# The embedding's bias by a spreading transfer instead of a one-row matmul

## The reference

```python
patches = x[:, idx, :].reshape(B, starts.shape[0], P * F)
return jnp.einsum('bnp,dp->bnd', patches, W) + b          # b has 512 values
h = h + _L0_attn_ref(_layernorm(h, axis=-1), ...)         # ternary weights, quantised activations
h = h + _L0_ffn_ref(_layernorm(h, axis=-1), ...)          # 16 experts
h = h + _L1_attn_ref(_layernorm(h, axis=-1), ...)         # causal attention
h = h + _L1_ffn_ref(_layernorm(h, axis=-1), ...)          # gated, with Hadamard rotations
```

## Time and profile before

| | |
|---|---|
| median of 3 runs | 303.21 us (302.82, 303.21, 305.16) |
| the profiled execution | 305.13 us, span of its instructions 303.3 us |
| PE, DVE, ACT, POOL busy | 277.0, 237.1, 145.0, 14.4 us |
| mean granted clock of PE over the span | 0.977 |

### The profile page before, as it was taken

One profiled execution on the slowest core, in us unless ns is written; L12 is line 12 of the kernel. 1 busy time (PEld: TensorE's weight loads), 2 busy tenths in 40 slices (PEclk: granted clock), 3 DMA queues, 4 the chain that ended last, 5 costly groups with the idle time before them and its releaser, 6 DMA issues. The chain is left out here.

```text
span 303.3 us, 4708 instructions
## 1 busy us (share of the span) xinstructions
PE 277.0 (91%) x1814; PEld 239.3 (79%) x1814; DVE 237.1 (78%) x438; ACT 145.0 (48%) x236; POOL 14.4 (5%) x32
## 2 busy tenths in 40 slices
PE   8988279959989999999999999987899999999993
PEld 3743144959988899999999988866799999999862
DVE  1789998593876999899989896698627896787683
ACT  2879550102844556556555423332128783673640
POOL 0200230010000000000000002300000000000000
PEclk9999789977999999999999999999999999999999
DMA  7940499912208466354520019276000000000003
GB/s 248 414 180 1 99 399 418 421 82 105 105 1 314 130 225 265 109 210 133 196 89 1 2 45 424 86 264 290 2 0 2 0 3 0 2 0 3 0 0 69
DMA packets 6567, 40.47 MB, mean 133 GB/s; under 512 B 1169, under 2 KB 1425, under 8 KB 5266
## 3 DMA queue, kind: packets, MB, share of 16 engines
q1 hardware_dynamic: 6546, 40.18, 35.1%
HBM read 39.13 MB, written 0.52 MB: 131 GB/s over the span
## 5 line engine op out<-in xcount | busy, mean ns | idle before, releaser
L870 PE MATMUL bank<-s_xt_hi,s_gu_hi 128*128 128x256 f32 x120 | 34.0, 283 | 0.0
L871 PE MATMUL bank<-s_xt_lo,s_gu_hi 128*128 128x256 f32 x120 | 33.9, 283 | 0.0
L872 PE MATMUL bank<-s_xt_hi,s_gu_lo 128*128 128x256 f32 x120 | 33.9, 282 | 0.0
L984 PE MATMUL bank<-s_xf_hi,s_f_hi 128*128 128x256 f32 x128 | 31.3, 283 | 0.1
L984 PE MATMUL bank<-s_xf_hi,s_f_lo 128*128 128x256 f32 x128 | 31.1, 281 | 0.0
L465 ACT CAST s_xt_hi<-bank 128x512 fp32r<-128x512 f32 x10 | 5.9, 587 | 42.4 <-PE bank L672 36.6
L984 PEld LDWEIGHTS bank<-s_xf_hi,s_f_hi 128*128 128x128 f32 x128 | 24.1, 188 | 0.7 <-ACT s_xf_hi L623 0.3
L984 PEld LDWEIGHTS bank<-s_xf_hi,s_f_lo 128*128 128x128 f32 x128 | 24.1, 188 | 0.3
L1480 DVE TENSOR_TENSOR s_f_lo<-s_ffn_raw,s_f_hi 128x1024 fp32r<-128x1024 f32 x16 | 19.6, 1225 | 6.1 <-ACT s_f_hi L596 6.1
L871 PEld LDWEIGHTS bank<-s_xt_lo,s_gu_hi 128*128 128x128 f32 x120 | 23.0, 191 | 0.2
L870 PEld LDWEIGHTS bank<-s_xt_hi,s_gu_hi 128*128 128x128 f32 x120 | 23.0, 191 | 0.3
(11 more groups left out here) (251 smaller groups left out, 731.0 us busy)
## 6 DMA issues: line engine op xcount, KB each, us to landing
s_moe_raw<-moe_gu SPq DMA_DIRECT2D x16, 768.0 KB, 5.9
s_ffn_raw<-ffn_w SPq DMA_DIRECT2D x4, 2048.0 KB, 9.9
s_moe_raw<-moe_dn SPq DMA_DIRECT2D x8, 768.0 KB, 4.4
s_big_raw<-att_w SPq DMA_DIRECT2D x4, 1024.0 KB, 8.3
s_big_raw<-down_w SPq DMA_DIRECT2D x1, 4096.0 KB, 25.1
s_l_raw<-l_w SPq DMA_DIRECT2D x1, 2560.0 KB, 15.1
out<-s_h SPq DMA_DIRECT2D x4, 128.0 KB, 2.3
s_tok_w<-tok_w SPq DMA_DIRECT2D x1, 256.0 KB, 2.7
```

What stands on the lines that cost most here:

```text
L870: pe.matmul(dst, w_hi, xt_hi[:, k, :], start=(k == 0), stop=False)
L871: pe.matmul(dst, w_hi, xt_lo[:, k, :], start=False, stop=False)
L872: last = pe.matmul(dst, w_lo, xt_hi[:, k, :], start=False, stop=(k == KC - 1))
L984: pe.matmul(tb(j, n)[:, 0:TOK], M[w][j][:, k, n * P:(n + 1) * P], M["xf_hi"][:, k, :], start=(w == "w_hi" and k == 0), stop=False)
```

## The change

The one-row tile `bias_row`, the one-row matmul, ACT's copy and their two semaphores go. SP loads the bias straight into the 128 x 512 tile `bias` by a transfer whose source row is repeated for each of the 128 partitions, as the third transfer, behind the patches and `tok_w`. DVE's `embedded(0)` waits for that transfer. Ahead of the embedding PE runs 14 spare matmuls in one piece (before: 5 and 2), behind it 13 (before: 26).

```diff
-        bias_row = sb("bias_row", [1, C])
...
         @block.sync
         def _(sp):
-            sp.dma_start(bias_row[:], tok_b).then_inc(ld_bias, 16)
             sp.dma_start(A["patches"][:], patches).then_inc(ld_in, 16)
             sp.dma_start(A["tok_w"][:], tok_w).then_inc(ld_tok, 16)
+            sp.dma_start(bias[:], tok_b.to_broadcast([P, C])).then_inc(ld_bias, 16)
             for m in range(4):
...
-            act.wait_ge(bias_done, 1)
-            act.copy(bias[:], bank[7][:]).then_inc(bias_ready, 1)
             abs_sum(0)
...
             pe.wait_ge(con_ready, 1)
-            early_warm(5)
-            pe.wait_ge(ld_bias, 16)
-            pe.matmul(bank[7][:], onesf[0:1, :], bias_row[:], start=True, stop=True).then_inc(bias_done, 1)
-            early_warm(2)
+            early_warm(14)
             pe.wait_ge(ld_tok, 16)
             pe.wait_ge(by_pos_ready, 1)
...
-            early_warm(26)
+            early_warm(13)
             weight_total(0, bank[3][:, 0:1])
...
-            dve.wait_ge(bias_ready, 1)
+            dve.wait_ge(ld_bias, 16)
```

More of the change, by code:

```diff
@@ L150, in tower @@
         k_swapped, v_swapped, gx_ready = sem("k_swapped"), sem("v_swapped"), sem("gx_ready")
-        by_pos_ready, bias_done, bias_ready, ld_rev = sem("by_pos_ready"), sem("bias_done"), sem("bias_ready"), sem("ld_rev")
+        by_pos_ready, ld_rev = sem("by_pos_ready"), sem("ld_rev")
         ld_tok = sem("ld_tok")
```

## The result

The changed kernel takes 307.26 us (median of 4 runs, 305.84 to 307.89), the kernel before 303.26 us on the same chip (302.82 to 305.16). The ratio, which comes with a 95% interval and is used throughout, is 1.0088 (1.0046 to 1.0131): slower, by a little under the 1% that I had called no change. The two medians lie further apart, 4.0 us (1.3%), and 307.26 us is outside the range of 301.7 to 304.8 us. The profiled execution took 307.89 us (span 306.1, mean granted clock 0.959) against 305.13 (303.3, 0.977): 2.8 us more.

A forecast was written before the change was run, and what follows sets the result against it. It took the start of `project(0, 1, 0)` at 17.49 us as the bound: up to 1.0 us gained from spare matmuls, 0.6 lost to late matrices, 0.1 taken off for the clock, so -0.3: 302.9 us, range 301.7 to 304.8.

The forecast's parts named there:

- The transfer: Load queue at the start: the 256 KB bias broadcast takes 1.7 us of it (bounds 0.63 and 2.4).
- D: Delay of the matrices loaded behind the bias: 1.7 - 0.4 = 1.3 us (0.2 to 2.0).
- The bias itself: Landing of the bias: at about 5.5 us, hidden by 0.5 us ahead of the first embedded tile at 6.0.
- Its clock: Embedding on PE: denser spare matmuls may bring 2.4 GHz earlier, so it takes 1.7 us instead of 3.41.
- rival B: PE's clock falls while it waits for the first matrix: +0.2 to +2.7 us, taken as +1.2, 304.4 us; chance 0.25.
- rival C: The bias broadcast is slower than `wsdp`'s: matrices 2.0 us or more late, +0.3 us or more, 303.6 us; chance 0.18.
- The formula 15.8 + D: Start of `project(0, 1, 0)` on PE: 15.8 us plus the matrices' delay, not before the spare matmuls end; 17.1 us forecast.
- Start of the embedding: Embedding on PE: starts near 4.0 us, 0.6 us earlier, as patches and `tok_w` are issued sooner.
- Spare matmuls behind it: PE behind the embedding: 13 instead of 26 take 1.4 to 2.7 us instead of 3.9; worth up to 1.0 us.
- Later loads: Matrices 2 and 3 and the experts: 1.3 us later too, but still in time; no cost.

The follow-up runs named there:

- experiment 2: The changed kernel with the bias stored as 128 rows in memory, so no source row repeats: 306.04 us, ratio 1.0072.
- experiment 3: The changed kernel with the bias as 128 rows in memory and 52 instead of 13 spare matmuls behind the embedding: 305.79 us, ratio 1.0053.
- experiment 11: Kernel before with 13 instead of 26 spare matmuls behind the embedding: 304.13 us; second kernel, also 4 instead of 8 between the projections: 304.18 us.
- experiment 13: Kernel before with 43 instead of 26 spare matmuls behind the embedding: 305.74 us, ratio 1.0072; with 34: 305.10 us, ratio 1.0052.
- experiments 4 and 5: 4: changed kernel with 7 and 26 spare matmuls as before, 305.19 us, 1.0044; 5: kernel before plus the bias broadcast into `wsdp`, 306.72 us, 1.0087.

## Why the prediction was wrong

**The step that failed is "The transfer".** It put D, the delay of the matrices, at 1.3 us, from 1.7 us of queue for a broadcast; measured are 2.55 and 2.50 us (9.89 and 9.88 against 7.34 and 7.38). The prediction's bound was 2.0. What was wrong in it is that I took the queue as one pipe and priced its mean. In the kernel before, the 16 engines deliver their parts of matrix 0 between 6.83 and 7.32 us; in the changed one they finish the bias between 4.24 and 6.67 us and matrix 0 between 7.75 and 9.87 (in the second profile between 7.37 and 9.86). The spread, once there, is passed on to what follows (matrix 1 between 10.25 and 12.39), and ACT waits for the last engine. The mean engine is later by 1.8 us in the first profile and by 1.2 in the second, around the 1.3 that I had forecast; the last is later by 2.5 in both. Of the Trainium skill's page "DMA: Bandwidth & Descriptors", section "Specifications", from which I had worked out D = 0.2, full rate for pieces of 512 bytes and more was seen with 128 separate rows in one execution (389 to 410 GB/s, experiment 2), and not in another with the same transfers (143 to 197, experiment 3) nor with one row read 128 times (70 to 86 and 127 to 197).

**"The bias itself"** failed with it: 6.7 us instead of 5.5, so it isn't hidden, and DVE's first tile is where it was. The faster embedding (2.09 us; I had left open 1.7 or 3.4) bought nothing.

**"Its clock" and rival B came true.** The upper clock came during the embedding, the 13 spare matmuls were done at 7.5 us, the gap was 4.51 us (3.7 forecast), and the 16 spare ones took 3.58 us (3.4 forecast). The Trainium skill, page "TensorE: Matmul & The Clock Gate", section "Loop structure matters more than you think", says that a long wait for a transfer between matmuls leaves the engine on the low clock; the trace agrees, 3.58 against 1.91 us with the gap covered. I gave this 0.25 and took +1.2 us for it with D = 1.3; with D = 2.5 both act at once, rival C's mechanism and B's. The formula 15.8 + D held: 18.24 by it, 18.36 measured with the gap covered. With the gap 18.84 to 19.43.

**"Start of the embedding"** held (forecast 4.0 us, measured 3.98). **"Spare matmuls behind it"** held on its own in the head (experiment 11, first kernel: 1.2 us or more earlier at `project(0, 1, 0)`; I had said up to 1.0), and nothing of it arrived in the median. **"Later loads"**: no wait of theirs was seen to grow, since DVE's sum of matrix 2 at 21.06 us came right behind its copy.

**What wasn't in the prediction:** that the end can follow the head by more than it moves. The changed kernel has 1.6 to 1.9 us at `project(0, 1, 0)` to hand down (first profiles against each other, and second), and the 24.4 us up to the 18 matmuls hand it down whole. The medians over all runs are 306.66 and 303.40, 3.3 us apart. The other 1.4 to 1.7 us fit the later clock: both profiles of the changed kernel are of the costliest kind (285.94 and 286.65 us from `project(0, 1, 0)` on), which is 1.6 to 2.4 above the cheapest (284.30 in the kernel before's second profile), and at least half of the kernel before's executions are by their times of the cheapest. That this shift of kinds is what separates the medians rests on two profiles of each kernel and is likely, not shown; how many of the changed kernel's ten runs were of which kind can't be read from their mean clocks. That a change of the spare matmuls alone can bring such a shift is shown by experiments 11 and 13: 1 of 12 in the first group with 13, with 13 and 4, and with 34 spare matmuls, against 73 of 114, in kernels with no transfer changed. It isn't the size of a delay that counts: with the transfer alone and with the order alone (0.7 to 1.2 us at the head) the share was 6 of 12 each. None of the fourteen other kernels, the changed one included, had as large a share as the kernel before. I had read the difference of 1.9 us between the profiled execution and the median as an offset to subtract; 1.5 us of it was the fall of the clock in the expert stage (285.82 against 284.30 us), and it belonged among the things the change could move.

**What stays open.** Why one engine or several fall 2 us behind when 128 more pieces, even of 64 bytes, stand in the queue ahead of the matrices, and not always (7.67 and 9.43 us in two profiles of one kernel); the runs exclude the bytes and the repetition as its only cause, and the loads from the constants on behind it. Single engines were late by 0.9 us with nothing added, too (15 by 7.35 us and the last at 8.24, experiment 13). How the loss divides between the transfer and the moved spare matmuls (experiments 4 and 5). And what ties the later falls of the clock to the place of the work: the stretch from 30 us on in which PE is busy less than half the time precedes the fall at 34 us, but filling it wasn't tried. No version tried beat the kernel before.

## What to carry to other kernels

A load that many engines share is as late as its last engine, so a transfer put ahead of a critical load is to be priced by the spread it leaves, not by its bytes over the mean rate; a row spread over the partitions by the queue made the matrices 2.5 us late, where the one-row matmul was not on the path. Spare matmuls that raise the clock earlier also finish earlier: count the gap that they leave before the next real input (here 4.51 us, which cost 0.5 to 1.1 us at `project(0, 1, 0)`). And before a difference of one or two microseconds is put down to the edited stretch, split each profiled execution at the first event that all kernels share behind the edit, and compare head with head and remainder with remainder: a change of the head can go with another course of the clock later. The mean clock of an execution doesn't make that split, since it adds up falls from everywhere.

## What the runs showed of the hardware that was not expected

- 256 KB loaded from one row of 2 KB read 128 times was complete at 6.55 to 7.15 us (five executions at full clock), from 128 separate rows at 4.84 and 5.24; both made the 1 MB load behind them as late (9.45 to 9.89 us in these seven executions; 7.34 to 8.27 with nothing added).
- With 128 pieces of 64 bytes (8 KB) added to the queue, a load of 1 MB behind them had its last engine at 7.65 us in one execution and 9.41 in another; six or one of 16 engines were late in other kernels by the same 2 us.
- The kernel before had 73 of its 114 times about 303.17 us (mean granted clock 0.979 or more) and 30 about 304.59 (0.968 or 0.969); taking 1.2 us out of its head left its median 0.8 us higher (ratio 1.0021, 0.9999 to 1.0043).
- In 17 profiles of 14 kernels with heads up to 3.3 us apart, what follows `project(0, 1, 0)` took 284.20 to 284.40, 285.74 to 285.82 or 285.94 to 286.65 us, by where the clock fell behind 30 us.
